# Compressed interaction network, one core: where the transposes and hidden-row copies of a period stand in the order of TensorE and ScalarE

## The reference

```python
for i in range(3):                       # W0: 39*39, W1 and W2: 100*39 rows; 200 columns each
    z = jnp.einsum('bmd,bnd->bmnd', x, hidden).reshape(B, -1, D)
    cur = jax.nn.relu(jnp.einsum('bcd,co->bod', z, Ws[i]) + bs[i][None, :, None])
    if i != 2:
        hidden, direct = cur[:, :100, :], cur[:, 100:, :]
    else:
        direct = cur
    finals.append(direct)
return jnp.sum(jnp.concatenate(finals, axis=1), axis=-1)
```

## Time and profile before

| | |
|---|---|
| median of 3 executions | 3346.16 us (3316.85, 3346.16, 3346.29) |
| the profiled execution | 3314.96 us |
| its span, first to last instruction | 3313.2 us |
| mean granted clock of PE | 0.922 |
| busy: PE, DVE, ACT | 88%, 82%, 49% of the span |

### The profile page before, as it was taken

One profiled execution on the slowest core, in us unless ns is written; L12 is line 12 of the kernel. 1 busy time (PEld: TensorE's weight loads), 2 busy tenths in 40 slices (PEclk: granted clock), 3 DMA queues, 4 the chain that ended last, 5 costly groups with the idle time before them and its releaser, 6 DMA issues.

```text
span 3313.2 us, 51577 instructions
## 1 busy us (share of the span) xinstructions
PE 2899.5 (88%) x17960; PEld 2844.1 (86%) x17960; DVE 2725.9 (82%) x2725; ACT 1619.3 (49%) x2212; POOL 0.7 (0%) x7
## 2 busy tenths in 40 slices
PE   3788888888888889998998899989998999899988
PEld 3788888888888888888888888888888888888888
DVE  5788888888888888888888888888887888788877
ACT  3454554555455454445445444444444444544444
POOL 0000000000000000000000000000000000000000
PEclk8899999999999998988889889889898898988988
DMA  8433433333434334333344343333333343334331
GB/s 192 112 102 103 107 90 104 105 90 108 113 103 111 99 91 109 100 90 90 104 117 103 92 109 99 90 91 105 105 91 92 104 106 91 90 95 111 94 90 52
DMA packets 230963, 335.32 MB, mean 101 GB/s; under 512 B 28072, under 2 KB 165268, under 8 KB 230804
## 3 DMA queue, kind: packets, MB, share of 16 engines
q1 hardware_dynamic: 230902, 334.50, 38.7%
HBM read 329.71 MB, written 6.60 MB: 102 GB/s over the span
## 4 chain that ended last, share of the span: by engine, by line
PE 72%; issue 9%; DVE 8%; ACT 8%; DMA 1%; SPq 1%; DVEq 0%; ACTq 0%
PE acc L734 49%; PE acc L735 22%; DVE z_low L411 6%; ACT z_high L588 4%; ACT hid L613 2%; ACT hid L611 1%; DVE z L395 1%; PE turned L743 1%; DVE z L407 1%; DMA xb<-x_by_unit 0%; DVE s L425 0%; DMA xb<-in_L_rec_b_dram 0%; ACT w_split L623 0%; ACT hid L610 0%; DMA z<-w_rows_again 0%
## 5 line engine op out<-in xcount | busy, mean ns | idle before, releaser
L734 PE MATMUL acc<-w_split,z_high 128*128 128x400 f32 (+1 forms) x8832 | 2866.9, 388 | 403.2 <-DVE z_low L411 401.6
L735 PE MATMUL acc<-w_split,z_low 128*128 128x200 f32 (+1 forms) x8832 | 2345.4, 266 | 0.0
L734 PEld LDWEIGHTS acc<-w_split,z_high 128*128 128x128 f32 (+1 forms) x8832 | 1783.3, 202 | 457.8 <-DVE z_low L411 399.7
L735 PEld LDWEIGHTS acc<-w_split,z_low 128*128 128x128 f32 (+1 forms) x8832 | 1811.6, 205 | 0.0
L588 ACT ACTIVATE z_high<-z 128x1024 fp32r<-128x1024 f32 (+2 forms) x1152 | 1179.1, 1024 | 1214.5 <-DVE z L407 488.6
L411 DVE TENSOR_TENSOR z_low<-z,z_high 128x1024 fp32r<-128x1024 f32 (+2 forms) x1152 | 1354.3, 1176 | 507.9 <-ACT z_high L588 507.6
L407 DVE TENSOR_TENSOR z<-hid,xb 128x1024 f32<-128x1024 f32 (+1 forms) x1024 | 1213.9, 1186 | 4.3 <-ACT hid L613 4.3
L610 ACT ACTIVATE hid<-turned 96x1024 f32<-96x1024 f32 (+1 forms) x130 | 131.0, 1008 | 423.2 <-PE turned L743 423.2
L613 ACT ACTIVATE hid<-turned 32x256 f32<-32x256 f32 (+1 forms) x390 | 144.1, 370 | 4.5
L395 DVE TENSOR_TENSOR z<-x_left,x_right 118x896 f32<-118x896 f32 x128 | 138.9, 1085 | 2.1 <-DMA x_right<-x_by_unit 2.1
L432 DVE SCALAR_TENSOR_TENSOR direct<-s,direct 128x400 f32<-128x400 f32 (+2 forms) x133 | 72.8, 547 | 18.4 <-DVE s L425 3.6
(11 more groups left out here) (26 smaller groups left out, 46.9 us busy)
## 6 DMA issues: line engine op xcount, KB each, us to landing
xb<-x_by_unit SPq DMA_DIRECT2D x384, 384.0 KB, 4.4
x_right<-x_by_unit SPq DMA_DIRECT2D x384, 136.5 KB
xb<-x_by_unit SPq DMA_DIRECT2D x384, 128.0 KB, 5.0
xb<-x_by_unit SPq DMA_DIRECT2D x128, 336.0 KB
xb<-x_by_unit SPq DMA_DIRECT2D x128, 84.0 KB
x_left<-x_by_unit SPq DMA_DIRECT2D x384, 19.5 KB
stage<-in_L_rec_W_dram SPq DMA_DIRECT2D x5, 600.0 KB, 9.4
x_by_unit<-stage SPq DMA_DIRECT2D x12, 160.0 KB, 3.2
```

The costliest lines, as they stand in the source:

```text
L734: nc.tensor.matmul(a[:, 0:2 * O], z_high[slot][0:rows, tok], w, start=(c == 0), stop=False, skip_group_check=True)
L735: last = nc.tensor.matmul(a[:, 0:O], z_low[slot][0:rows, tok], w[:, 0:O], start=False, stop=(c == chunks - 1), skip_group_check=True)
```

## The change

DVE's and SP's programs stay as they are. On PE, the two transposes move from behind the matmuls of part b to the end of the period before, ahead of them. On ACT, `dup` moves from behind `highs` of part b to the end of the period before, ahead of it; and `hidden` moves from behind `highs` of part b+1 to behind `highs` of part b+2 and `second_half2`. The second period (r, d = 0, 1) has its own order in the middle and keeps it; the last one keeps its end.

```diff
@@ scalar: period @@
                 highs(base, slot(0), P, group_chunks(0))
                 if second:
                     second_half(0, 2, base - 1)
-                else:
-                    dup(a1, 2, ended(n - 1))
                 highs(base + 1, slot(1), P, group_chunks(1))
                 if second:
                     dup(0, 2, ended(0))
                     high_piece(2, 1)
-                else:
-                    hidden(a1, 2, ended(n - 1), 1 - par)
                 highs(base + 2, slot(2), P, group_chunks(2))
                 if second:
                     hidden(0, 2, ended(0), 0)
                     high_piece(2, 2)
                 else:
                     second_half2(base - 1)
+                    hidden(a1, 2, ended(n - 1), 1 - par)
                 highs(base + 3, slot(3), P, group_chunks(3))
...
                 highs(base + q + 3, slot(q + 3), P, group_chunks(3))
+                if not final:
+                    dup(a, b, ended(n))
@@ tensor: period @@
                 pe.wait_ge(s_in, ended(n - 1))
                 multiply(1, base, slot(0), 0)
-                if not second:
-                    transpose(a1, 2, ended(n - 1))
                 multiply(1, base + 1, slot(1), 1)
...
                 multiply(2, base + q + 3, slot(q + 3), 3)
+                if not final:
+                    transpose(a, b, ended(n))
```

More of the change, by code:

```diff
@@ L773, in period @@
                 a, b = layers_ended(r, d)
-                a1 = 1 if final else 0
                 def slot(p):
```

## The result

| | before | after |
|---|---|---|
| median of the executions | 3341.53 us (4, 3316.85 to 3346.29) | 2793.91 us (4) |
| the profiled execution, its span | 3314.96, 3313.2 us | 2793.52, 2791.7 us |
| ratio after to before | | 0.8373, 95% interval 0.832 to 0.8426 |

The change makes the kernel 16% faster. One of the four executions after took 3064.5 us at a mean granted clock of 0.751 and is left out of the ratio: no profile of it exists, so its cause stays open, the prediction's "I expect all executions close together" does not hold for it, and its time lies in the band of rival 2. The others lie at 2793.14, 2793.52 and 2794.31. The forecast was 2813, in a range of 2790 to 2905.

The account below looks back on a forecast made before the run. It took a stall in the ring of ACT, PE and DVE as the bound, with DVE next. DVE's 507.6 us of waits less some 5 gave -502 from 3315.0: 2813 us, range 2790 to 2905.

Parts of the forecast that it names:

- rival 2: On PE, small waits keep the clock down and make PE the bound: 2860 to 3090 us, chance 0.07.
- These three are one stall: DVE's 507.6 us wait for `z_high`, ACT's 423.2 for the transposes and PE's 401.6 for `z_low` share one cause.
- The walk: One changed period timed from the product of b+2: `lows` of b+3 comes 3.7 us earlier, DVE never waiting.
- 0.2 us after it is ready: DVE's spare time at `lows` of b+3: DVE arrives at 6.4, `z_high` is there at 6.2.
- Costs at nothing: The earlier transposes, the earlier `dup` and the loads of fields were each claimed to cost nothing.
- The next bound: Without the stall DVE binds at 21.0 us a period, PE close behind at 20.6; the period was 25.1.
- The sum: DVE's 507.6 us of waits less some 5 gives -502, from the profiled 3315.0: 2813 us.
- lower bound of 2790: The forecast's low end, if a quarter of DVE's other 80 us of idle time, mostly at the start, goes too.
- rivals 2 and 3: The second of them: small waits in nine parts keep PE at half clock, 3400 us and up, chance 0.03.
- The guess on the spread: Both clock levels of the kernel before come from the stall; without it all executions should lie close together.
- Rival 1: ACT's block ahead of and including `highs` of b+3 is too long, so DVE waits: 2830 to 2910 us, chance 0.10.
- d - 0.2: DVE's wait in every period if ACT's block starts d late; 1 us late gives 0.8 x 126 = 100 us.

Follow-up runs that it names:

- e1: The kernel before with only ACT's `hidden` moved behind `highs` of b+2 and `second_half2`, transposes and `dup` left in place: 2818.11 us, ratio 0.8445 to the kernel before.
- e2: The changed kernel with `hidden` put back behind `highs` of b+1, transposes and `dup` still early: 2902.89 us, ratio 0.8701 to the kernel before.
- e8: The changed kernel with ten PE transposes instead of two at each place: 2825.5 us, ratio 0.8456 to the kernel before.
- e3: The changed kernel with two more ACT copies (96x512 and 96x256) behind L610 that nobody waits for: 2847.48 us, ratio 0.8532 to the kernel before.
- e5: The changed kernel with one more ACT copy (32x256) behind L610 that nobody waits for: 2801.61 us, ratio 0.8384 to the kernel before.
- e9: The changed kernel with `directs` on DVE behind the product of b+4 instead of ahead of it: 2763.82 us, ratio 0.8289 to the kernel before.

## Why the prediction was right

- *The stall.* "These three are one stall" holds: with the order changed, 507.6, 423.2 and most of 401.6 us went together (2.5, 7.4 and 62.6 us are left), and e1 and e2 show that the ready copy queued behind `hidden` was its larger half. The prediction didn't split the two; it read both from one timeline. Moving `hidden` is what counted most, not PE's earlier transposes.
- *The walk.* It said 1.3, 2.6, 5.2 and 6.4 for `highs` of b+2, L610, `highs` of b+3 and `lows` of b+3; the trace has 1.31, 2.49, 5.08 and 6.40 in an ordinary period. "0.2 us after it is ready" was sized too small: the rows after, e3 and e5 give 0.31 to 0.36. The rows of before had 1.08 us between `highs` of b+2 and L598, and after it is 0.97, so ACT's block is 3.77 and not 3.90 us.
- *Costs at nothing.* `dup` waits 0.6 us for `sums` (77.3 us at 129 times) and nobody behind it is late: `highs` of b still waits 0.95 us for its product. PE waited for `dup` at no steady transpose. Loads cost 0.7 us in the whole run (2.8 against 2.1 us of waits).
- *The next bound.* 21.0 for DVE and 20.6 for PE was right: 21.1 measured, PE 0.6 below it (e8).
- *The sum* took off 19 us too little: 2813 against 2793.5 for the profiled execution. DVE's idle time fell by 587.3 - 81.3 = 506 us, near the -502. What the sum left out is that DVE's busy time fell too, by 2725.9 - 2710.4 = 15.5 us. A row of DVE says 1.22 us where the next one starts after 1.135; ahead of a wait the last 0.09 us count as busy, so a wait in the list is 0.09 us smaller than what is lost. The walk had that (3.74 us for this period, where the row of the wait says 3.65), the sum from the list didn't: 0.09 us at one long wait in each of 128 periods is 11.5 us, at all 161 waits that went 14.5. What remains of the 15.5, 1 to 4 us, isn't traced further. The result lies near the forecast's lower bound of 2790, but not for that bound's reason, that a quarter of DVE's other idle time goes too: it was 79.7 us and is 78.8.
- *The clock.* With the long wait gone the granted clock is at 1.00 from 115 to 2700 us, though PE's weight loads still wait 218 times there, 0.3 us each and 0.5 at the longest. For the profiled executions that rules out rivals 2 and 3, and it speaks against carrying over the Trainium skill's rule on short idle times (TensorE: Matmul & The Clock Gate, "A second HAM failure mode: psum-queue depth-cycling"). (Rival 2's own working gives 2813 + 0.3 x 126 = 2851 as its lower end, where its heading has 2860.) The guess on the spread also holds where both kernels ran side by side: the kernel before lay between 3312.98 and 3348.12 us in eleven executions of one chip, the changed one between 2792.96 and 2795.86 in six.
- *Rival 1* was the live one. Its mechanism is shown by e3 and e5: from one to the other, 0.39 us more in the block cost 0.36 us more a period, close to the full price that the rival's "d - 0.2" asks, from 0.35 us on instead of 0.2.

**Open:** how the gain divides into the wait itself and the half-clock pairs behind it wasn't tried, since one doesn't come without the other here.

## What to carry to other kernels

When a strictly ordered engine waits for another, look at what is queued behind the waiting instruction: here a finished product lay 4.7 us behind it. Putting an instruction that isn't urgent behind the copy that is, cured most of the stall without making any input earlier. Then walk one period through, since the next margin (0.35 us on an engine that is 59% busy) is in no busy share; and when two engines show 97%, add a little work to one to learn which is the bound.

## What the hardware showed that I had not expected

- A DVE instruction with two inputs beside GpSimd's `tensor_tensor` of 128x400 (1.05 us) took 2.07 us instead of 1.22, while `lows` of b+3 beside GpSimd's `tensor_scalar` (1.78 us) kept its 1.09. GpSimd's `tensor_scalar` had itself started 0.27 to 0.38 us behind the start of DVE's product of b+4 and ended 1.06 to 1.08 us behind that product's end, in all 111 periods read; so its 1.78 us seem to hold a wait for the product (GpSimd's times in a profile are rough). The Trainium skill, SBUF — State Buffer ("SBUF: two separate sides"), describes the port pair that the two engines share as an exclusive lock. The 2.07 us and the late end of `tensor_scalar` fit that; that `lows` of b+3 kept its 1.09 us with over 0.7 us of `tensor_scalar` still to run doesn't.
- The same 128x200 addition on DVE was followed after 0.49 us by an instruction that needs its result, and after 0.27 us by one that doesn't. In 125 periods that is 27 of the 30 us that e9 brought.
